# A fixed slot of 11 steps for the layer-norm and projection work inside the edge-count stage of a GNN kernel

## What is computed

```
x = x + L0_gnn(layernorm(x), src, dst, ...)       # attention over edges, 12 heads of 64
x = x + L0_ffn(layernorm(x)[None], ...)[0]
x = x + L1_gnn(layernorm(x), ...)
x = x + L1_ffn(layernorm(x)[None], ...)[0]

# L0_gnn
hv = h.reshape(n, H, DIN)
ft = einsum('nhd,od->nho', hv, W)                 # projection
a1 = sum(ft * attn_l, -1);  a2 = sum(ft * attn_r, -1)
e  = leaky_relu(a1[src] + a2[dst], 0.2)
...                                               # softmax over the edges of a node, weighted sum
res = einsum('nhd,od->nho', hv, W_res)
out = relu(agg + res)
```

## Time and profile before

| | |
|---|---|
| median of 3 runs | 1070.89 us (1070.14 to 1073.16) |
| the profiled execution | 1073.16 us, of which its span is 1071.4 us |
| TensorE busy | 982.3 us, 92% of the span |
| VectorE busy | 605.2 us, 56% |
| ScalarE busy | 287.8 us, 27% |
| stage of the counts | from 8.8 us to 171.3 us |
| tiles 1 to 4 of the counts | 19.4 us each |
| tile 5 | 17.3 us and then 1.55 us without work on TensorE |
| tiles 7 and 8 | 12.4 us each |

### The profile page before, as it was taken

The page is one execution under the profiler, slowest core; times in us unless marked ns, Lnnn a source line. Parts: engine busy times, 40 slices in busy tenths (PEclk is TensorE's granted clock), DMA queues, the critical chain, the costliest instruction groups (busy, mean ns, idle before and its releaser), DMA issues. The chain is left out here.

```text
span 1071.4 us, 15579 instructions
## 1 busy us (share of the span) xinstructions
PE 982.3 (92%) x5652; PEld 794.5 (74%) x5652; DVE 605.2 (56%) x1251; ACT 287.8 (27%) x782; POOL 59.9 (6%) x114
## 2 busy tenths in 40 slices
PE   7999998999999999955499993999999999999996
PEld 4777677999999999934266652666997557878774
DVE  7887897999999999985022225552211112233231
ACT  2434244444455544222000000211111113210000
POOL 2000000000000000021112210000000000000000
PEclk9999998999999999978699996999999999999999
DMA  3100010000000001235632242314200001100001
GB/s 117 37 1 1 11 43 1 24 25 23 37 33 23 23 23 60 108 125 221 212 118 96 96 150 113 128 50 158 81 1 1 0 1 75 70 29 29 26 13 50
DMA packets 24007, 65.25 MB, mean 61 GB/s; under 512 B 4200, under 2 KB 8052, under 8 KB 23824
## 3 DMA queue, kind: packets, MB, share of 16 engines
q1 hardware_dynamic: 21504, 54.21, 14.1%
q0 software_dynamic: 2080, 10.23, 2.8%
q10 hardware_dynamic: 368, 0.07, 0.0%
HBM read 47.74 MB, written 16.76 MB: 60 GB/s over the span
## 5 line engine op out<-in xcount | busy, mean ns | idle before, releaser
L800 PE MATMUL O<-X,masks 125*125 125x264 f32 x1200 | 281.1, 333 | 2.9 <-DVE masks L945 2.9
L797 PE MATMUL O<-X,CSR 125*125 125x132 f32 x1080 | 245.5, 227 | 0.0
L800 PEld LDWEIGHTS O<-X,masks 125*125 125x125 f32 x1200 | 223.0, 188 | 3.1 <-issue 3.1
L945 DVE SCALAR_TENSOR_TENSOR masks<-a2b,NA,CSR 125x375 fp32r<-125x375 f32 (+1 forms) x360 | 212.7, 648 | 9.6 <-PE O L800 7.3
L797 PEld LDWEIGHTS O<-X,CSR 125*125 125x125 f32 x1080 | 205.8, 191 | 0.0
L1868 DVE SCALAR_TENSOR_TENSOR UL<-pw,dinv,UH 125x768 fp32r<-125x768 f32 x20 | 20.4, 1019 | 111.2 <-ACT UH L1791 111.2
L1648 PE MATMUL pw<-W 128*125 128x384 f32 x240 | 81.4, 497 | 1.0 <-ACT W L1784 1.0
L418 PE MATMUL pc<-ohs_a,ohd 125*125 125x512 f16 x375 | 77.8, 347 | 1.6 <-DVE ohs_a L621 1.6
L1648 PE MATMUL pw<-region,xr_or_h 128*125 128x384 f32 x240 | 77.6, 486 | 0.0
L149 POOL TENSOR_TENSOR rstd<-rstd,minus_half 125x1 f32<-125x1 f32 x40 | 25.4, 636 | 847.4 <-DVEq L143 847.4
L621 DVE TENSOR_SCALAR ohs_a<-iota,srcf 125x1250 f16<-125x1250 f16 x128 | 69.7, 544 | 0.0
(11 more groups left out here) (237 smaller groups left out, 1381.5 us busy)
## 6 DMA issues: line engine op xcount, KB each, us to landing
a2b<-a_rows SPq DMA_DIRECT2D x12, 610.4 KB
W<-in_L_ffn_W SPq DMA_DIRECT2D x4, 1152.0 KB, 6.0
WM<-in_L_ffn_W SPq DMA_DIRECT2D x4, 1152.0 KB, 9.3
xr_or_h<-in_x SPq DMA_DIRECT2D x10, 375.0 KB
region<-in_x SPq DMA_DIRECT2D x2, 1875.0 KB
z_rows<-region SPq DMA_DIRECT2D x10, 375.0 KB
region<-y_rows SPq DMA_DIRECT2D x10, 375.0 KB
x_rows<-xr_or_h SPq DMA_DIRECT2D x10, 375.0 KB
```

What stands on the lines that cost most here:

```text
L797: nc.tensor.matmul(O[0:P, bank, d - d0, 2 * DP:4 * DP], CSR[:, s, d * P:(d + 1) * P], X[:, buf, s, 4:6, :].rearrange("p k d -> p (k d)"), ...
L800: ins = nc.tensor.matmul(O[0:P, bank, d - d0, 0:4 * DP], kept, X[:, buf, s, 0:4, :].rearrange("p k d -> p (k d)"), start=s == 0, stop=s == ...
L945: nc.vector.scalar_tensor_tensor(masks[:, s, 0:(d1 - d0) * P], a2b[:, buf, d0 * P:d1 * P], NA1[:, s, bass.ds(h, 1)], CSR[:, s, d0 * P:d1 * ...
```

## The change

The list of slot starts and `slot_of` go. Every slot has 11 steps, from n = 0, so the slots begin at n = 0, 11, 22, 33, 44, 55, 66, 77, 88, 99, 110, 121. VectorE's `z_of` moves from place 9 to place 10. Places 0, 2 and 5 (TensorE and ScalarE) and 6 and 8 (VectorE) stay, and so does all that is tied to n or to (t, c).

```diff
-            SLOT_START = [(k * WIN + 1) // 2 - PRE for k in range(2 * NT + 2)]
+            SLOT = 11
...
-            def slot_of(n):
-
-                k = max(k for k, first in enumerate(SLOT_START) if first <= n)
-                return k, n - SLOT_START[k]
...
                     for n, (t, c) in enumerate(STEPS):      # in the queues of TensorE, ScalarE and VectorE
-                        k, at = slot_of(n)
+                        k, at = divmod(n, SLOT)
...
                             if at == 8:
                                 scale(k)
-                            if at == 9:
+                            if at == 10:
                                 z_of(k)
```

## The result

The changed kernel takes 1077.82 us (median of 4 runs, 1076.46 to 1078.92), the kernel before 1070.67 us (4 runs, 1070.14 to 1073.16). The ratio is 1.0061 with a 95% interval of 1.0041 to 1.0082: slower by 7.15 us as the medians go, by 4.4 to 8.8 us as the interval has it. The forecast was 1077.6 us.

What follows compares the result with a forecast made beforehand. TensorE was taken to bound the count stage. Boundary holes of 6.74 us less 0.07 at the second turn_z gave +6.7 us, on the median of 1070.89 a forecast of 1077.6 us, range 1074.2 to 1081.5.

Steps and rivals of the forecast that it cites:

- TensorE bounds the stage: Count stage: TensorE works 19.21 of 19.37 us in a two-projection tile; VectorE has 3.75 us to spare, 2.40 in tile 1.
- The count copy loses its cover at tiles 1, 2, 3 and 5, and keeps part at tile 4: First count step of tiles 1 to 5: TensorE waits for ScalarE's copy of the counts, 6.74 us in sum.
- The second turn_z: TensorE's waits there for ScalarE's copy_zt: 1.98 us in six slots replaces 2.05 us, a change of -0.07.
- z_of later costs nothing: VectorE's z comes about three steps later for row tile 1; costed at nothing, at most 6.8 us without VectorE's lead.
- the 25 that was estimated: Row tile 1 after the change: VectorE's z estimated done before 25 us on the timeline.
- about 27.8: Row tile 1 after the change: predicted time in us at which TensorE first uses z, at n = 22.
- its cover is VectorE's lead: Count stage: VectorE runs up to eight steps ahead in time, hiding a later z; without it, at most 6.8 us.
- Nothing soaks the delay up: Behind tile 5, TensorE is busy for all of 14.21 and 12.35 us, so no later wait absorbs the delay.
- from the gather on every interval should be as long as before: Profile sign: after the count stage ends 6 to 7 us later than 171.3, later intervals keep their length.
- The clock does not fall in the holes: TensorE's clock stays at 1.00 in the new boundary waits, as after the 1.55 us wait at tile 6.
- The three rivals: VectorE bounds, 1068.8 us, chance 0.04; wait soaked up, 1071 to 1075, 0.12; clock falls, 1082 (once) to 1095, 0.06.
- the fourth, z late: Rival: TensorE's turn_z waits for VectorE's z, some fraction of 6.8 us, 1080 to 1084 us; chance 0.04.

Runs made afterwards that it cites:

- the shift of one step: Kernel before with every slot start one count step later, slot lengths and z_of place unchanged: 1078.72 us, ratio 1.0067.
- Both closings: Second turn_z and its copy at place 3 instead of 2: in the kernel after 1074.81 us, ratio 1.0034; in the kernel before 1068.28 us, ratio 0.9971.
- two small moves: Kernel before with second turn_z and its copy at place 3, and project(9, 1) with its take moved from n = 114 to 124: 1066.61 us, ratio 0.9957.

## Why the prediction held, point by point

- **TensorE bounds the stage.** Shown. Changing VectorE's order alone costs nothing measurable, changing the order on TensorE and ScalarE alone costs everything, and VectorE's wait for the ring grew as TensorE's holes did.
- **The count copy loses its cover at tiles 1, 2, 3 and 5, and keeps part at tile 4.** Shown at each place. Worked out 1.55, 1.55, 1.87, 0.22, 1.55, in sum 6.74; measured from the windows and timelines 1.55, 1.55, 67.86 - 65.94 = 1.92, 0.22 and 1.55, in sum 6.79. That alignment and nothing else in the slots does it is shown by the shift of one step.
- **The second turn_z: six holes of 0.33 in place of five of 0.33 and four of 0.1.** Shown for the count (the waits list six, before five) and for the size, by closing them. The four of 0.1 are too short for the view of waits. Both closings gave a little more than the sum, 2.14 for 1.98 and 2.34 for 2.05. Most of that stands in the rows: the two transposes behind such a hole take 0.24 us (27.81 to 28.05, before) in place of 0.22 (27.70 to 27.92, with the hole closed).
- **A term that the sum left out: the work right behind a hole.** The prediction priced the idle time alone. The first count step behind each of the five new holes takes about 0.05 us longer, 0.25 in all, and the second `turn_z` gives back 2.34 - 2.14 = 0.20 and not 0.07. So the parts as measured are 6.79 + 0.25 - 0.20 = 6.84, beside the 6.85 of the stretch; the 6.7 came so near because errors of both signs partly cancel.
- **z_of later costs nothing.** Shown twice, by z_of back at 9 and by VectorE's list alone. For row tile 1, z is begun at 24.07 and done at 24.75, before the 25 that was estimated; TensorE reads it at 28.41. (The prediction's "about 27.8" for that leaves out `project(0, 1)`, 1.33 us, which stands ahead of it. That only adds to the margin.) My estimate that its cover is VectorE's lead holds from tile 1 on; in tile 0 there is hardly any, which the change doesn't touch since it moves the reader as well.
- **Nothing soaks the delay up.** The gather stage starts 182.65 - 176.59 = 6.06 us later in the profiled executions, which is the 6.85 of the stretch less 0.78 that tile 0 happened to be shorter. The sign "from the gather on every interval should be as long as before" did not hold in these two executions: VectorE's `gdeg<-deg` starts at 488.49 before and 493.70 after, 5.21 apart, and `ar<-al` at 749.57 and 754.06, 4.49 apart. That is not the delay being absorbed: in the run with VectorE's list alone, which has no delay to absorb, the same two come at 487.03 and 746.74, 1.46 and 2.83 early. And the medians are 7.15 apart.
- **The clock does not fall in the holes.** Shown for holes of 1.55 us and, at tile 3, of 1.92: 1.00 in them and behind them. The section "HAM oscillation — how this bites in real kernels" of the Trainium skill's page "TensorE: Matmul & The Clock Gate", cited in the prediction, tells of bursts of about 2 us that are shorter than the waits between them. Here about 19 us of work lie between holes of less than 2, so no run tests that rule, and the prediction's word that the trace disagrees with it says too much.
- **The median.** 1077.82 for 1077.6. That it is this close is luck: the four runs spread over 2.5 us and the interval of the difference goes from 4.4 to 8.8. The agreement that counts is that of the stretch and of each hole. The three rivals would have given 1068.8, 1071 to 1075, and 1082 or more; the fourth, z late, 1080 to 1084.

## What to carry to other kernels

Where one engine bounds a stage, a schedule written by hand is as good as what stands right ahead of each wait of that engine: here 1.75 us of other matmuls ahead of a wait of 1.55, and one step of misalignment costs 7 to 8 us without any added work. Before evening out a schedule, list for every hard wait what covers it before and after, in the order of the queues of both engines (ScalarE's `take` ahead of the copy made one hole 0.37 longer). The same list shows what the old schedule left: here two small moves, found from it, made the kernel 0.4% faster than the kernel before.

## What the runs showed of the hardware that was not expected

The clock of TensorE differs between executions at the same place in the program, and this is about as large as the smaller effects measured here. After the idle 2.92 us at the end of the stage, the kernel before began the gather with its first two matmuls at 0.55 and 0.31 us and a granted clock of 0.50 over the next 8.75 us:

```profile
176.59 0.55 PE L800 MATMUL O<-X,masks 125*125 125x264 f32 x1 [2.92 <-DVE masks L945]
176.94 0.31 PE L804 MATMUL O<-X,CSR 125*125 125x132 f32 x1
```

The kernel after began with matmuls of 0.33 and 0.22 us, went over to the longer ones half a microsecond later, and averaged 0.61:

```profile
182.65 0.36 PE L795 MATMUL O<-X,masks 125*125 125x264 f32 x1 [2.92 <-DVE masks L940]
182.85 0.22 PE L799 MATMUL O<-X,CSR 125*125 125x132 f32 x1
182.91 0.33 PE L795 MATMUL O<-X,masks 125*125 125x264 f32 x1
183.08 0.22 PE L799 MATMUL O<-X,CSR 125*125 125x132 f32 x1
183.14 0.45 PE L795 MATMUL O<-X,masks 125*125 125x264 f32 x1
183.38 0.31 PE L799 MATMUL O<-X,CSR 125*125 125x132 f32 x1
```

(0.61 - 0.50) x 8.75 is 1.0 us; of the distance between the two executions 6.06 - 5.21 = 0.85 is gone by 489 us. Another 0.72 us goes between there and 750 us, where the granted clock also falls below 1.00 in both (0.74 from 470 to 520 us); which part of it is the clock's isn't shown. At the very start nine matmuls take 3.38 us where the same nine take 1.76 later, although the granted clock of that stretch is listed as 1.00: at the start the durations say more than the clock row. VectorE isn't what they wait for: it writes the one-hots of a step in 0.62 us, and these three steps start at 8.83, 9.92 and 10.96.

```profile
8.83 3.38 PE L413 MATMUL pc<-ohs_a,ohd 125*125 125x512 f16 x9 [1.61 <-DVE ohs_a L616]
...
22.27 1.76 PE L413 MATMUL pc<-ohs_a,ohd 125*125 125x512 f16 x9
```

That stretch ended at about 12.7 us after the change and past 13 before it, which puts tile 0 0.78 us apart in the two traces. The run with z_of at place 9 has the same list on TensorE as the kernel after, but its next count step was still slow, and it reached the end of tile 0 at 24.84 in place of 23.88. So the execution alone can do this, whatever the order. First the kernel after, then that run:

```profile
12.68 0.75 PE L413 MATMUL pc<-ohs_a,ohd 125*125 125x512 f16 x3
```

```profile
12.72 1.30 PE L413 MATMUL pc<-ohs_a,ohd 125*125 125x512 f16 x3
```

The stretch compared above begins behind tile 0 and ends ahead of the gather stage, and so holds none of these differences.
